# Macaron block on one core: where the values' products stand in TensorE's attention step

## The reference

```python
x = x + 0.5 * ffn(layernorm(x), ...)
x = x + attn(layernorm(x), ...)
x = x + 0.5 * ffn(layernorm(x), ...)

def attn(x, W_down, tokeys, toqueries, tovalues, W_unify, b_unify):   # 16 heads of 16
    xd = (x @ W_down).reshape(b, t, h, s)
    keys    = einsum('bthk,hik->bthi', xd, tokeys) * s ** -0.25
    queries = einsum('bthk,hik->bthi', xd, toqueries) * s ** -0.25
    values  = einsum('bthk,hik->bthi', xd, tovalues)
    attn = softmax(einsum('bqhs,bkhs->bhqk', queries, keys))
    out = einsum('bhqk,bkhs->bqhs', attn, values).reshape(b, t, e)
    return out @ W_unify + b_unify
```

## Time and profile before

| what | value |
|---|---|
| median of 3 runs | 3113.79 us (3112.69 to 3118.69) |
| the profiled execution, its own time | 3127.16 us |
| its span | 3125.4 us |
| mean granted clock of PE | 0.939 |
| first and last `times_v` (attention's second passes) | about 759 to 2476 us |

### The profile page before, as it was taken

The page is one execution under the profiler, slowest core; times in us unless marked ns, Lnnn a source line. Parts: engine busy times, 40 slices in busy tenths (PEclk is TensorE's granted clock), DMA queues, the critical chain, the costliest instruction groups (busy, mean ns, idle before and its releaser), DMA issues. The chain is left out here.

```text
span 3125.4 us, 53454 instructions
## 1 busy us (share of the span) xinstructions
PE 2804.5 (90%) x17263; PEld 1677.0 (54%) x17263; DVE 2136.0 (68%) x3460; ACT 1865.1 (60%) x3505; POOL 553.6 (18%) x506
## 2 busy tenths in 40 slices
PE   5999999937989989989989999899899769999987
PEld 3888998822334333333333333343343248889987
DVE  6554456627878878878877878788789275444575
ACT  5444456512767766767756767677677554445564
POOL 3354124420000000000000000000000034431353
PEclk9999999966989999999989989999899979999998
DMA  5211124314133142232232321331411142111242
GB/s 173 55 47 48 46 63 131 93 37 109 26 91 63 35 96 49 58 77 54 80 62 50 87 59 34 89 69 35 95 35 35 39 140 61 54 40 49 79 132 71
DMA packets 161993, 214.47 MB, mean 69 GB/s; under 512 B 26168, under 2 KB 123392, under 8 KB 161792
## 3 DMA queue, kind: packets, MB, share of 16 engines
q1 hardware_dynamic: 153600, 201.39, 25.4%
q0 software_dynamic: 8192, 10.57, 1.1%
HBM read 146.79 MB, written 64.05 MB: 67 GB/s over the span
## 5 line engine op out<-in xcount | busy, mean ns | idle before, releaser
L1527 DVE TENSOR_REDUCE at_mxc<-at_pb 128x2 f32<-128x1024 f32 x1024 | 1222.1, 1220 | 270.5 <-PE at_pb L1346 259.7
L1460 ACT ACTIVATE at_ex<-at_pd 128x512 f32<-128x512 f32 x2048 | 1095.4, 597 | 490.2 <-PE at_pd L1357 482.8
L1357 PE MATMUL at_pd<-at_qa,at_ka 50*128 50x512 f32 x2048 | 574.2, 472 | 80.1 <-DMA at_qa<-at_mparts 65.6
L1357 PEld LDWEIGHTS at_pd<-at_qa,at_ka 50*128 50x128 f32 x2048 | 251.7, 189 | 610.9 <-issue 253.1
L768 DVE TENSOR_TENSOR f_ml_hl<-f_ml_h,f_ml_hh 128x512 fp32r<-128x512 f32 (+1 forms) x384 | 266.7, 696 | 447.4 <-ACT f_ml_hh L844 382.0
L1366 PE MATMUL at_po<-at_ex,at_va 128*32 128x512 f32 x4096 | 559.9, 619 | 0.0
L841 ACT ACTIVATE f_ml_h<-f_ml_pL,b1T 128x512 f32<-128x512 f32 (+1 forms) x384 | 243.9, 635 | 453.0 <-PE f_ml_pL L895 384.0
L1346 PE MATMUL at_pb<-at_ka,at_qa 48*128 48x512 f32 x2048 | 453.2, 460 | 20.2 <-DVE at_mxc L1527 18.8
L910 PE MATMUL f_ml_pA<-f_wh,f_ml_hh 128*128 128x256 f32 (+1 forms) x1408 | 409.8, 291 | 1.1 <-DVE f_ml_hl L768 1.0
L913 PE MATMUL f_ml_pA<-f_wh,f_ml_hl 128*128 128x256 f32 (+1 forms) x1408 | 401.8, 285 | 0.0
L912 PE MATMUL f_ml_pA<-f_wl,f_ml_hh 128*128 128x256 f32 (+1 forms) x1408 | 401.8, 285 | 0.0
(11 more groups left out here) (125 smaller groups left out, 2833.8 us busy)
## 6 DMA issues: line engine op xcount, KB each, us to landing
f_wraw<-in_L_ffn_w SPq DMA_DIRECT2D x128, 256.0 KB, 2.7
at_scr<-at_parts SPq DMA_DIRECT2D x64, 512.0 KB
at_qa<-at_scr SPq DMA_DIRECT2D x128, 128.0 KB, 4.7
at_ka<-at_scr SPq DMA_DIRECT2D x64, 256.0 KB, 4.7
f_ro_xr<-in_L_attn_x SPq DMA_DIRECT2D x16, 512.0 KB, 3.9
f_ml_xr<-in_L_attn_x SPq DMA_DIRECT2D x16, 512.0 KB, 4.2
x<-f_ml_yo SPq DMA_DIRECT2D x16, 512.0 KB, 3.9
at_xr<-x SPq DMA_DIRECT2D x16, 512.0 KB, 4.7
```

Source lines behind the costliest of these rows:

```text
L1357: eng.matmul(pd[n % RING][:, :], ka[g][rows, p, kt * P:(kt + 1) * P], qa[g][rows, qh, p, :], start=True, stop=True).then_inc(s_full.sem, 1)
L1460: eng.activation(ex[t % 2][:, j, :], pd[n % RING][:, :], ACT.Exp).then_inc(s_free[n % RING].sem, 1)
L1527: eng.tensor_reduce(mxc[:, t // NT, kh, t % NT::NT], pb[kh][:, :].rearrange("p (e k) -> p e k", e=2), AX.X, ALU.max).then_inc(s_mx.sem, 1)
```

## The change

The order of PE's step becomes: two `for_exp`, `times_v`, two `for_exp`, the first `for_max`, the side product, the second `for_max`. The ring's numbers follow: a step's four exponential tiles are numbered first, then its side product. ACT's step becomes four exponentials and then the evacuation of the side product. DVE's, POOL's and SP's steps stay as they are.

```diff
@@ phase
-                        tiles = self.ready = [self.ring.take() for _ in range(2)]
+                        tiles = self.ready = [self.ring.take() for _ in range(GH)]
...
-                    if tiles:
-                        tiles += [self.ring.take() for _ in range(2)]
                     do.step(b, par, g, t, coming, tiles, done, a, side, not ends, last)
@@ PE step
                     for j in range(2 if tiles else 0):
                         for_exp(self.ring, *coming, j, tiles[j])
+                    times_v(self.ring, b, par, g, t, done)
+                    for j in range(2, GH if tiles else 2):
+                        for_exp(self.ring, *coming, j, tiles[j])
                     if ahead:
                         for_max(b1, g1, t, 0)
                     if a:
                         side_product(self.ring, a)
                     if ahead:
                         for_max(b1, g1, t, 1)
-                    for j in range(2, GH if tiles else 2):
-                        for_exp(self.ring, *coming, j, tiles[j])
-                    times_v(self.ring, b, par, g, t, done)
@@ ACT step
-                    for j in range(2 if tiles else 0):
+                    for j in range(GH if tiles else 0):
                         exponentials(self.ring, t + 1, j, tiles[j])
                     if a:
                         side_out(self.ring, a)
-                    for j in range(2, GH if tiles else 2):
-                        exponentials(self.ring, t + 1, j, tiles[j])
```

## The result

The changed kernel takes 3355.16 us (median of 4, 3350.39 to 3362.37), the kernel before beside it 3116.24 us: a ratio of 1.0769, interval 1.0745 to 1.0794. That is 239 us more; 174 were forecast, and the time lies inside the range.

What follows compares the result with a forecast made beforehand. PE was taken as the bound, with DVE not far behind. Terms of 91 + 9 + 13 + 3 + 58 = 174 us on the median of 3113.8 gave 3288 us, range 3208 to 3365.

Steps and rivals of the forecast that it cites:

- The values' product of a half waits for the copy.: Attention, steps 8 and 0: times_v waits for DVE's copy behind two reductions; 55 x 1.65 = 91 us.
- f no longer waits, then 2.92 us to V(9).: Step 8 in attention: the transposes lose their copy wait, a 28.4 us gain already held in the 91 us.
- The seven DMA waits cover the stall before them and begin 1.34 us later.: Waits for the maxima's DMA, g = 2, step 15: earlier delay covered, 1.34 us more each, 9 us in all.
- V follows closer on its exponentials.: Plain attention steps: times_v waits for its last exponential, 2.61 to about 2.73 us; 13 us, last unit some 3 more.
- The waiting terms together.: Attention's waits without the clock: 91 + 9 + 13 + 3 = 116 us.
- The rival of 3230 us: Attention: the stall costs its waits, 116 us, but the clock stays full; chance 0.21.
- The clock.: Attention: PE's pauses of some 2.2 us lower its clock after seven in ten; 0.7 x 55 x 1.5 = 58 us.
- a rival at a chance of 0.10: Attention: the clock stays low for longer, two dips after each of 55 pauses, 165 us, 3395 us; chance 0.10.
- a pause alone: Single PE pause in attention: whether the clock dips was left unsettled, bounds 0 to 94 us.
- The rule on pauses.: Skill's warning covers only longer PE pauses; by it the clock costs zero and the time is 3230 us.

Runs made afterwards that it cites:

- copy-first kernel: Changed kernel with DVE's values_out moved ahead of both maxima in steps 7 and 15; 3121.88 us, ratio 1.0015 to the kernel before.
- filled kernel: Changed kernel, DVE's order kept, plus two identity products on the whole array before the second exponential product of steps 0 and 8; 3230.15 us, ratio 1.0356.

## Why the prediction was right, and where its size was off

- *The values' product of a half waits for the copy.* Right in mechanism and size in a plain step. Forecast: V(8) 4.86 us after V(7), a pause of 2.2 us, waits of 110 to 130 us in some 55 places. Measured: 4.79 us (1488.07 to 1492.86), 2.11 us, 122.8 us in 60. The distance grew by 2.18 us over the plain step of before; where step 7 has a side product it grew by 1.7 to 2.5 us. Putting the copy first took the wait all away, moving it by one reduction took away 64% of it.
- *f no longer waits, then 2.92 us to V(9).* The wait is gone, but in the copy-first kernel and in the filled one the distance is 3.10 us (1458.62 to 1461.72): a step with f is bound by more than PE's own pieces. What holds the 0.18 us was not tried.
- *The seven DMA waits cover the stall before them and begin 1.34 us later.* Right in mechanism: with no stall they grew from 65.6 to 75.1 us, the forecast 9 us. In the new order they shrank to 51.9 us, 7.4 each and not 8 to 9. That the work between them and the chain's start took longer there fits this; how much of it was stall and how much low clock was not separated.
- *V follows closer on its exponentials.* Right in sign, half in size: plain steps went from 2.61 to 2.67 us, not to 2.73.
- *The waiting terms together.* Forecast 116 us. With the clock held up by filling 112 us remain, 106 by the estimate above. The rival of 3230 us was the stall alone; with the clock held up the kernel takes 3230.15. The mechanism is confirmed by that; the match to the last microsecond is luck, since the filling overshoots and the comparison's kernel before loses clock of its own.
- *The clock.* This is the term that was mis-sized. It was entered as a dip after seven pauses in ten, at 1.5 us: 0.7 x 55 x 1.5 = 58 us. The filled kernel gives 125 us, some 133 by the estimate above. Both factors were too low, the price more so: 52 dips against 38, at 133 / 52 = 2.6 us each. The price came from the expert stage, where 1.7 us were lost after a pause of 2.18 us and the clock was low for 3.4 us; in attention a dip lasts about twice as long. The better row was there: the 18 us window at 0.79 after a wait in attention itself, which I kept for a rival at a chance of 0.10. The truth lies between that rival (165 us) and my term.
- *What the earlier trace rows said of a pause alone.* I read the pair at 1688.47, 0.49 us long, as full speed after the first pause, and called the case not settled. The reading was wrong. The clock fell at 1688.80, 0.7 us after the first pause had ended, and the second pause lies inside the low stretch:

```profile
1688.80:1695.60 6.80, 4.19 (x18) 1.41 (x16) 2.95 (x4) 1.98 (x4) 0.00 (x0) 0.50 0.02 5
```

At the other pause of this kind in attention (2.12 us, ending at 1245.1) the clock fell as the pause ended. Both were in the trace of the kernel before and would have spoken for a dip after nearly every pause.

- *The rule on pauses.* The Trainium skill ("TensorE: Matmul & The Clock Gate", section "Why this matters for your kernels") warns of longer pauses than these. That shorter ones cost no clock, as the prediction took from it for a rival, is not borne out here: pauses of 2.1 us took the clock of attention from 0.96 to 0.88, and filling them with products gave it back.

## What to carry to other kernels

When products are moved on one engine, look at which other engine's instruction they hand to and take from, and where that stands in the other's order: a copy that stood behind two reductions was nearly harmless while its reader came a step later, and cost 7.7% when the reader moved up. A short stall of TensorE in the bottleneck should be priced at the wait and, where it is as long as the 2.1 us here, at as much again or more for the slower clock behind it (133 us beside 106 in this kernel); stalls of 0.74 us cost next to no clock. The price of a dip is best read in the same stage. Filling the stall with dummy products tells the two costs apart, if the filling does not outlast the stall.

## What was not expected of the hardware

- After the same 2.1 to 2.2 us of standstill the clock was low for 3.4 us in the expert stage (490.8 to 494.2 us of the kernel before) and for 6.8 us on average in attention. Why is not shown.
- Useless products that only fill a stall made the kernel 125 us faster. With the filling on 50 rows of the array 28 low stretches of the clock were left, with those on all 128 rows 10 (four products) and 9 (two). The fillings also differ in the pause they leave, 0.66 us on average (56 times) against none and 0.19 us (33 times), so it is not shown that the rows made the difference.
- Pauses of 0.74 us on average, 60 of them, left the clock of attention at 0.95, where the kernel before has 0.96.
